# A three-part transformer layer on eight cores: another order of VectorE, ScalarE and GpSimd around feed-forward 1, and of P1 in the output projection

## The reference

```python
# feed-forward (1 and 3)
x_prev = concatenate([zeros, x[:, :-1]], axis=1)
xr = mu_r * x + (1.0 - mu_r) * x_prev
xk = mu_k * x + (1.0 - mu_k) * x_prev
r = sigmoid(xr @ W_r.T)
k_act = square(relu(xk @ W_k.T))
out = r * (k_act @ W_v.T)
# attention block: layer norm, low-rank Q, K, V, causal softmax, then
h = hidden_states + ctx @ out_U @ out_V + out_b
x2 = layernorm(h, ln2_g, ln2_b)
out = h + gelu(x2 @ fc1_U @ fc1_V + fc1_b) @ fc2_U @ fc2_V + fc2_b
```

## Time and profile before

| | |
|---|---|
| median of three runs | 1157.29 us (1156.97 to 1312.77) |
| the profiled execution | 1159.1 us, span of its slowest core (2) 1157.5 us |
| spans of the cores 0 to 7 | 1153.5, 1150.0, 1157.5, 1153.0, 1152.4, 1152.4, 1154.3, 1148.9 us |
| mean granted TensorE clock, core 2 | 0.979 |
| busy on core 2 | TensorE 1051.0 us, VectorE 531.0, ScalarE 534.1, GpSimd 190.6 |
| chain that ended last | TensorE 78%, VectorE 8%, ScalarE 6%, issue 3%, DMA 2% |
| feed-forward 1, first K matmul to last V matmul | 27.88 to 215.2 us |
| projection, OP0 to the last F | 625.4 to 721.1 us |

### The profile page before, as it was taken

One profiled execution on the slowest core, in us unless ns is written; L12 is line 12 of the kernel. 1 busy time (PEld: TensorE's weight loads), 2 busy tenths in 40 slices (PEclk: granted clock), 3 DMA queues, 4 the chain that ended last, 5 costly groups with the idle time before them and its releaser, 6 DMA issues.

```text
span 1157.5 us, 15164 instructions; the slowest of 8 cores (1148.9 to 1157.5 us)
## 1 busy us (share of the span) xinstructions
PE 1051.0 (91%) x5500; PEld 445.6 (38%) x5500; DVE 531.0 (46%) x1011; ACT 534.1 (46%) x646; POOL 190.6 (16%) x189
## 2 busy tenths in 40 slices
PE   1997799999899898888998988999999999999995
PEld 1443344433333333333433433444444444444442
DVE  6466685554544435455467944003021125744511
ACT  2425434356667677777655324333333354241320
POOL 2030321300000002110012213691000000033113
PEclk9999899999999999999998988999999999999998
DMA  8964247712110107540058845973030014131211
GB/s 165 206 179 124 47 120 155 160 24 55 19 19 1 19 1 109 84 64 1 1 165 200 113 68 83 205 150 73 1 73 1 1 37 77 34 109 73 55 55 72
DMA packets 89733, 92.60 MB, mean 80 GB/s; under 512 B 66112, under 2 KB 70336, under 8 KB 88384
## 3 DMA queue, kind: packets, MB, share of 16 engines
q0 software_dynamic: 20112, 52.74, 24.7%
q1 hardware_dynamic: 69552, 38.92, 13.7%
HBM read 91.94 MB, written 16.78 MB: 94 GB/s over the span
## 4 chain that ended last, share of the span: by engine, by line
PE 78%; DVE 8%; ACT 6%; issue 3%; DMA 2%; SPq 1%; POOL 1%; POOLq 0%; ACTq 0%; DVEq 0%
PE ub L865 10%; PE db L1335 9%; PE db L1301 9%; PE db L352 9%; PE db L366 8%; PE db L378 8%; PE ct L1029 5%; PE sd L994 5%; ACT AT L1004 4%; PE db L1273 4%; PE ub L873 3%; PE db L1314 2%; PE db L1288 2%; PE ub L913 2%; DVE st L417 2%
## 5 line engine op out<-in xcount | busy, mean ns | idle before, releaser
L1004 ACT ACTIVATE AT<-sd 128x1024 bf16<-128x1024 f32 (+1 forms) x320 | 265.0, 900 | 126.6 <-PE sd L994 126.5
L1384 ACT ACTIVATE HM<-db,csts 128x512 bf16<-128x512 f32 x128 | 80.7, 684 | 138.9 <-PE db L1301 138.9
L994 PE MATMUL sd<-Qr,Kr 64*128 64x512 bf16 (+3 forms) x640 | 95.3, 349 | 33.8 <-ACT AT L1004 33.2
L1335 PE MATMUL db<-HM,f2U 128*128 128x512 bf16 x512 | 120.3, 379 | 1.6 <-ACT HM L1384 1.6
L1301 PE MATMUL db<-P,f1V 128*128 128x512 bf16 x512 | 120.3, 379 | 0.1
L1029 PE MATMUL ct<-AT,VA 128*64 128x512 bf16 (+3 forms) x640 | 90.1, 359 | 6.1 <-DVE AT L1011 5.9
L1335 PEld LDWEIGHTS db<-HM,f2U 128*128 128x128 bf16 x512 | 49.8, 98 | 62.6 <-issue 3.3
L1301 PEld LDWEIGHTS db<-P,f1V 128*128 128x128 bf16 x512 | 49.9, 98 | 60.9 <-issue 0.8
L1273 PE MATMUL db<-Wo,CN 128*128 128x512 bf16 x256 | 64.1, 417 | 9.8 <-ACT P L1372 9.7
L378 PE MATMUL db<-wv,KAa 128*128 128x512 bf16 x256 | 57.5, 386 | 15.3 <-DVE tta L406 15.3
L1472 DVE CAST P<-db 128x1024 bf16<-128x1024 f32 x4 | 4.9, 1225 | 138.4 <-PE db L1335 138.4
(11 more groups left out here) (153 smaller groups left out, 1306.5 us busy)
## 6 DMA issues: line engine op xcount, KB each, us to landing
S<-xs POOLq DMA_DIRECT2D x32, 512.0 KB, 11.1
xs<-X SPq DMA_DIRECT2D x4, 2048.0 KB, 9.5
x_out<-S SPq DMA_DIRECT2D x16, 512.0 KB, 2.6
wr<-wrT POOLq DMA_DIRECT2D x4, 1024.0 KB, 18.0
X<-x_in SPq DMA_DIRECT2D x2, 2048.0 KB, 14.0
f1V<-fc1V POOLq DMA_DIRECT2D x16, 256.0 KB, 4.0
f2U<-fc2U POOLq DMA_DIRECT2D x32, 128.0 KB, 6.8
X<-x_in SPq DMA_DIRECT2D x4, 512.0 KB, 7.8
```

The source lines that it names most:

```text
L994: m = pe.matmul(SD[q % 2][:, TB * s + off:TB * (s + 1)], Kr[p % 2][64 * s:64 * s + 64, 128 * i:128 * (i + 1)], Qr[p % 2][64 * s:64 * s + 6 ...
L1004: act.activation(c3(AT[q % 4])[:, :, off:TB], c3(SD[q % 2])[:, :, off:TB], AF.Exp, scale=0.125)._wait_ge(a_qk, q + 1).then_inc(a_exp, 1)
L1335: m = pe.matmul(DB[2 + p2 // 2][:, TB * (p2 % 2):TB * (p2 % 2 + 1)], f2U[ic // 8][:, 512 * (ic % 8) + 128 * p2:512 * (ic % 8) + 128 * (p2 ...
L1384: m = act.activation(HM[i % 4][:, TB * e:TB * (e + 1)], DB[job_db[("H", b, i)]][:, TB * e:TB * (e + 1)], AF.Gelu_apprx_tanh, bias=scol("fc ...
```

## The change

- Feed-forward 1: `tt` gets a third buffer, and `dve_kv` waits for the add three tiles back rather than two. kv(b,0) goes ahead of the mixing of the next block, kv(b,1) into `dve_mix_k`, kv(b,2) between the mixings, kv(b,3) into `dve_mix_r`, in all of blocks 0 to 2. Statistics A of block b+1 go between the squares of block b, statistics B of block b-1 behind them, for b = 1 and 2.
- ScalarE: the A rows of block 3 move from among the relus of block 2 to behind its second sigmoid; the B rows of block 1 with them.
- GpSimd: the adds of blocks 1 and 2 wait for XK of the next block, as those of block 0 already did. The loads of the merges move from block 3 to block 2 (when R(2) is done), without the wait for XR(3).
- TensorE: 14 matmuls of the identity with the first columns of `wk0`, into DB0, behind the first transposes.
- `dve_aff1(0)` keeps its place behind the mixings of block 3.
- Projection: ScalarE runs `act_p1` directly behind the rows of tile 7, 11 and 15, ahead of the deviation of the next tile; VectorE takes the scale of tile 7 (11, 15) directly behind the tile itself.

```diff
-    f0.tt = [at("tta%d" % i, 1024, F32, 176 + 4 * i) for i in range(2)]
+    f0.tt = [at("tta%d" % i, 1024, F32, (176, 180, 192)[i]) for i in range(3)]
...
-        n = 4 * b + t
-        if n >= 2:
-            dve.wait_ge(F.add, n - 1)
+        n, k = 4 * b + t, len(f.tt)
+        if n >= k:
+            dve.wait_ge(F.add, n - k + 1)
...
-    def dve_mix_r(dve, F, f, b):
+    def dve_mix_r(dve, F, f, b, kv=None):
...
+        if kv:
+            dve_kv(dve, F, f, b - 1, kv)
         dve.tensor_tensor(XR[:, :, 1:TB], XR[:, :, 1:TB], Z[:, :, 0:TB - 1],
...
+        pe.wait_ge(t_ev, 1)
+        pe.wait_ge(d_wk[0], 16)
+        for i in range(14):
+            pe.matmul(DB[0][:, 0:TB], ident[:, :], wk0[:, 0:TB], start=True, stop=True)
...
+            for p in range(4):
+                act_relu(act, F0, f0, b, p)
+            if b < NB - 1:
+                act_sig(act, F0, f0, b, 0)
+                act_sig(act, F0, f0, b, 1)
                 act_sd_a(act, b + 1)
                 act_z(act, "A", b + 1, range(4))
+                if b:
+                    act_sd_b(act, b - 1)
+                    act_z(act, "B", b - 1, range(4))
+                act_sig(act, F0, f0, b, 2)
+                act_sig(act, F0, f0, b, 3)
...
+        for b in range(1, NB - 1):
             for p in range(4):
                 dve_sq(dve, F0, f0, b, p)
+                dve_stats_a(dve, b + 1, p)
+            for k in range(4):
+                if k == 2:
+                    dve_rs_a(dve, b + 1)
+                dve_stats_b(dve, b - 1, k)
+            dve_rs_b(dve, b - 1)
+            dve_kv(dve, F0, f0, b, 0)
+            for k in range(4):
+                dve.wait_ge(d_tr[k], 16 * (group("A", b + 1) + 1))
+            dve_mix_k(dve, F0, f0, b + 1, kv=1)
+            dve_kv(dve, F0, f0, b, 2)
+            dve_mix_r(dve, F0, f0, b + 1, kv=3)
+            if b == 2:
+                dve_aff1(dve, 0)
...
-                if b == 3 and t == 0:
+                if b == 2 and t == 0:
                     pool.wait_ge(F0.r, 12)
                     pool.dma_start(qVT[:, :], dram["qVT"]).then_inc(d_qV, 16)
                     pool.dma_start(kVTb[:, :], dram["kVTb"]).then_inc(d_kV, 16)
                     pool.dma_start(vVT[:, :], dram["vVT"]).then_inc(d_vV, 16)
-                    pool.wait_ge(F0.xr, 4)
                     pool_pair_weights(pool, 0)
+                if b == 3 and t == 0:
                     pool.wait_ge(F0.k, 16)
...
-                if b == 0 and t == 0:
-                    pool.wait_ge(F0.xk, 2)
+                if b < NB - 1 and t == 0:
+                    pool.wait_ge(F0.xk, b + 2)
...
-            if t + 1 < NT:
+            border = t in (7, 11, 15)
+            if not border:
                 act_op_sd(act, t + 1)
-            if t in (8, 12):
-                act_p1(act, t // 4 - 2)
             act_zu(act, t, (o_nm, t + 1), t, rsC, nmC)
-        act_p1(act, 2)
+            if border:
+                act_p1(act, t // 4 - 1)
+                if t + 1 < NT:
+                    act_op_sd(act, t + 1)
...
-            if t:
+            if t and t not in (8, 12):
                 dve_op_rs(dve, t - 1)
             if t >= 2 and t + 6 < NT:
                 dve_hs(dve, t + 6)
-        dve_op_rs(dve, NT - 1)
+            if t in (7, 11, 15):
+                dve_op_rs(dve, t)
```

More of the change, by code:

```diff
@@ L401, in dve_kv @@
     def dve_kv(dve, F, f, b, t):
-        n = 4 * b + t
-        if n >= 2:
-            dve.wait_ge(F.add, n - 1)
+        n, k = 4 * b + t, len(f.tt)
+        if n >= k:
+            dve.wait_ge(F.add, n - k + 1)
         dve.wait_ge(F.sig, n + 1)
-        dve.scalar_tensor_tensor(f.tt[t % 2][:, :], DB[2 * t % 4 + 1][:, :], 0.5, f.rt[t % 2][:, :],
+        dve.scalar_tensor_tensor(f.tt[n % k][:, :], DB[2 * t % 4 + 1][:, :], 0.5, f.rt[t % 2][:, :],
                                  ALU.mult, ALU.mult)._wait_ge(F.v, n + 1).then_inc(F.kv, 1)
@@ L410, in pool_add @@
         xt = f.x(4 * b + t)
-        pool.tensor_tensor(xt, xt, f.tt[t % 2][:, :],
+        pool.tensor_tensor(xt, xt, f.tt[(4 * b + t) % len(f.tt)][:, :],
                            ALU.add)._wait_ge(F.kv, 4 * b + t + 1).then_inc(F.add, 1)
@@ L650, in act_phase0 @@
         for b in range(NB):
[L651 to L668, removed]
+            for p in range(4):
[3 more added lines that the diff above has]
+                act_sig(act, F0, f0, b, 1)
                 act_sd_a(act, b + 1)
                 act_z(act, "A", b + 1, range(4))
[L671 to L674, removed]
+                if b:
[3 more added lines that the diff above has]
+                act_sig(act, F0, f0, b, 3)
+            else:
+                act_sd_b(act, b - 1)
+                act_sig(act, F0, f0, b, 0)
+                act_z(act, "B", b - 1, [0, 1])
+                act_sig(act, F0, f0, b, 1)
+                act_z(act, "B", b - 1, [2, 3])
                 act_va(act, 0)
-            act_sig(act, F0, f0, b, 2)
-            act_sig(act, F0, f0, b, 3)
+                act_sig(act, F0, f0, b, 2)
+                act_sig(act, F0, f0, b, 3)
         act_sd_b(act, NB - 1)
@@ L701, in dve_phase0 @@
         dve_mix_r(dve, F0, f0, 0)
-        for b in range(NB):
+        for p in range(4):
+            dve_sq(dve, F0, f0, 0, p)
+        for k in range(4):
+            dve_stats_a(dve, 1, k)
+        dve_rs_a(dve, 1)
+        dve_kv(dve, F0, f0, 0, 0)
+        for k in range(4):
+            dve.wait_ge(d_tr[k], 16 * (group("A", 1) + 1))
+        dve_mix_k(dve, F0, f0, 1, kv=1)
+        dve_kv(dve, F0, f0, 0, 2)
+        dve_mix_r(dve, F0, f0, 1, kv=3)
+        for b in range(1, NB - 1):
             for p in range(4):
@@ L706, in dve_phase0 @@
                 dve_sq(dve, F0, f0, b, p)
[L707 to L748, removed]
@@ L749, in dve_phase0 @@
-            if b == 0:
-                dve_mix(dve, 1, dve_mix_r)
+                dve_stats_a(dve, b + 1, p)
+            for k in range(4):
+                if k == 2:
[3 more added lines that the diff above has]
+            dve_kv(dve, F0, f0, b, 0)
+            for k in range(4):
+                dve.wait_ge(d_tr[k], 16 * (group("A", b + 1) + 1))
+            dve_mix_k(dve, F0, f0, b + 1, kv=1)
+            dve_kv(dve, F0, f0, b, 2)
@@ new lines, in dve_phase0 @@
+            dve_mix_r(dve, F0, f0, b + 1, kv=3)
+            if b == 2:
+                dve_aff1(dve, 0)
+        b = NB - 1
+        for p in range(4):
+            dve_sq(dve, F0, f0, b, p)
+            if p < 3:
+                dve_stats_b(dve, b - 1, p)
+            if p == 2:
+                dve_stats_b(dve, b - 1, 3)
+        dve_rs_b(dve, b - 1)
+        dve_aff1(dve, b - 2)
+        for u in early:
+            dve_unit(dve, u)
+        dve_aff1(dve, b - 1)
+        for t in range(4):
+            dve_kv(dve, F0, f0, b, t)
+            if t:
+                dve_stats_b(dve, b, t - 1)
@@ L758, in dve_phase0 @@
             dve_unit(dve, u)
[L760 to L763, removed]
     F0.hz = sem("f0_hz")
```

## The result

The changed kernel takes 1146.56 us (median of the runs; before 1157.29), a ratio of 0.9909 with an interval of 0.989 to 0.9929: 10.7 us faster, where 18.2 were forecast, and just outside the range. The medians are over all executions; the ratios leave out those in which the cores of one die ran slower at a lower granted clock. The profiled execution took 1146.03 us; its slowest core is core 4, span 1144.5 (spans of the eight: 1134.2 to 1144.5).

A forecast was written before the change was run, and what follows sets the result against it. TensorE is busy 1051.0 of 1157.5 us, so only its stands and half-clock time can be won. Feed-forward 1's 3.4 plus the projection's 14.8 take 18.2 off 1157.3: forecast 1139 us, bounds 1127 to 1146.

The forecast's parts named there:

- what comes in its place: Feed-forward 1: new per-block chain and block 3's wait leave a gain of 3.4 us, not 17.6; merge loads cost 0.3.
- Rival (c): Clock falls 2.8 us before V0 (2.9) and block 3's transposes land 2.4 later beside loads: 1144 us, chance 0.11.
- the exclusion: Feed-forward 1: two-input bf16 VectorE sum and GpSimd add exclude each other; XR ready T+14.7 (T: XK ready), otherwise T+12.3.
- the period: Feed-forward 1: each block's chain, from XK ready to the next, takes 43.0 us (41.4 without the exclusion), TensorE's 41.44.
- the wait for G's eviction: Block 3: merges wait for VectorE's evictions of G, R(3,2) at 188.5; stand of about 9 us, slow clock taken 2.3.
- the projection: Projection: P1 is out before OP10 and OP14 need it, so two stands and slow matmuls go: 15.0 us, taken as 14.8.
- the old kv wait: Feed-forward 1: V(1,2) finds kv(1,0) done, so its 15.3 us stand and 1.5 us of slow matmuls go.
- the warm-up: Before K0: fourteen matmuls make K0 and R0 end 2.9 us earlier, but V0 waits for wv, so gain 0.2.
- (a): Feed-forward 1: two-input sums and GpSimd don't exclude one another; period 41.4, gain 9.1 + 14.8: 1133.4 us, chance 0.24.
- (b): Feed-forward 1: GpSimd's adds cost VectorE next to nothing; R(3,2) waits 1.5, gain 16.1 + 14.8: 1126 us, chance 0.09.
- (e): Projection: P1 still waits at the borders, held by something other than its place; 3.4 gained alone: 1154 us, chance 0.03.
- (d): Everywhere: a denser TensorE stream is granted a lower clock; 1.7% pays back the 18.2, 3% gives 1170 us, chance 0.03.

The follow-up runs named there:

- e3: Changed kernel with GpSimd held until block 3's four A transposes have landed before it issues the five merge loads: 1134.83 us, ratio 0.9812.
- the halves: Projection edits alone on the kernel before: 1140.91 us, ratio 0.9865; changed kernel with the projection's old order: 1160.2 us, ratio 1.0025.
- e7: e3 with VectorE's evictions of G, qb and Wq ahead of the affines of blocks 0 and 1: 1129.56 us, ratio 0.9773.
- e1: Kernel before with only the projection edits (borders in ScalarE's and VectorE's order): 1140.91 us, ratio 0.9865.
- e9: e7 with three of a block's four GpSimd adds waiting for XR, and without the fourteen warm-up matmuls: 1124.03 us, ratio 0.9721.
- e6: Changed kernel with one merge load (qVT) beside block 3's A transposes and four held behind them: 1137.7 us, one execution.
- e5: Changed kernel with three merge loads beside block 3's A transposes and two held behind them: 1143.11 us, one execution.
- e10: e7 with three of a block's four GpSimd adds waiting for XR, and 28 warm-up matmuls for 14: 1124.71 us, ratio 0.9726.

## Why the prediction was wrong, and where it was right

**The step that failed** is in the paragraph on what comes in its place: "plus 0.3 for the loads of the merges, five issues that POOL now makes at the end of R2 beside the last transposes". The place and the collision were seen; the size was wrong. It measured 11.2 us at the end (e3). On core 4, 10.5 of them stand in the rows: 8.9 us of later transposes and mixing and 2.8 us of slow matmuls in V(2,3), less the 1.16 that K3 waited in e3. V3 starts 10.0 later there, 10.5 in the mean of the cores (204.9 against 194.4). Rival (c) had the same collision at 2.4 us, and its other half (V0) at 2.9; its 1144 is the nearest to the result, and its two sizes were off as well: the transposes' 2.4 was 6.0 to issue (12.44 against 6.46) and 8.9 to the start of the mixing. The step priced the loads as issues on GpSimd's queue (2.8 us for five), not as traffic beside a latency-bound chain. It also followed the delay to XK(3) alone. The delay reached TensorE before that, at V(2,3), through kv(2,1), which the change itself had put inside that mixing: on core 4 V(2,3) starts at 162.64, and K3, behind it at 168.92, finds XK(3) ready since 167.16. The trace shows this path; no run took kv(2,1) out of the mixing, so how much of the 11.2 it adds over a late XK(3) alone is not measured.

**The sum** from forecast to result: 18.2; projection 0.6 more than its 14.8; the loads 11.2 less; and 3.1 more, which is what remains, to 10.7. It is good to some 2 us, the difference left open between the halves. The remainder is in block 3, where V3 starts 3.3 us ahead of the forecast once the loads are gone. e3 is the prediction's own case without the loads, and on core 2, for which it was worked out, step by step, it reads:

| step of the prediction | forecast | core 2 of e3 |
|---|---|---|
| XK(3) ready, T3 | 157.4 | 157.44 |
| XR ready (exclusion, T+14.7) | 172.1 | 171.70 |
| G out (T+30.5) | 187.9 | 186.86 |
| R(3,2) | 188.5 | 187.50 |
| V3 starts | 197.9 | 194.62 |

**Confirmed**: the exclusion, and by it the period; the wait for G's eviction. **Mis-sized**: the 2.3 us of slow clock behind G. The timeline of TensorE there:

```profile
171.95 3.61 PE L366 MATMUL db<-wr,XRa 128*128 128x512 bf16 x16 [0.29 <-DVE XRa L481]
178.33 0.61 PE L829 MATMUL ub<-kVTb,qVT 128*128 128x128 bf16 x8 [2.76 <-ACT krla L387]
178.77 5.30 PE L366 MATMUL db<-wr,XRa 128*128 128x512 bf16 x16
186.52 0.34 PE L834 MATMUL ub<-bcst,kVTb 128*128 128x1 bf16 x8 [2.44 <-DVE Gs L915]
187.22 0.38 PE L844 MATMUL ub<-Gs,qUT 128*128 128x128 bf16 x4 [0.36 <-DVE qbias L917]
187.50 3.61 PE L366 MATMUL db<-wr,XRa 128*128 128x512 bf16 x16
```

The stop is in two parts, 2.76 before G and 2.44 before qb. The clock fell in the first, the slow 16 matmuls (5.30 for 3.61) ran inside the time in which TensorE would have waited for G anyway, and R(3,2) was at full pace. Lateness of R(3,2) against an undisturbed K3 is 8.2 us, forecast 9; the clock cost nothing on this core, nor on cores 3 and 6. On the other five cores of e3, the two slowest among them, R(3,2) itself was slow, at 4.7 to 5.3 for 3.61: 1.1 to 1.7 us, still under the 2.3. The changed kernel is like those five on seven cores: on core 4 the second stop is 4.13, and R(3,2) behind it was slow.

**Right**: the projection (15.4 measured alone, 15.0 worked out, 14.8 taken); the old kv wait gone; the warm-up worth 0.2 at most, with wv as the bound on the six cores where V0 waits for it. Only the reason was too kind: K0, forecast 2.9 shorter, stays slow on six cores, two of which never wait for wv, since the fall comes back in the stand behind the matmuls; so that the term came out is in part luck. And V0's own slow matmuls, taken as none, came on two cores. "The shortest stand after which the clock fell was 2.7" misreads its trace: 2.7 us is how long TensorE had stood when the clock fell, in a stand of 4.51. Nor is it a bound: on core 2 of the changed kernel V0 takes 15.65 behind a stand of 2.19, and in e7 matmuls are slow behind 1.33. **Rivals**: (a) falls with the halo sum's 2.22 us beside an add, (b) with the scalings, 7.22 beside three adds and 3.00 beside one; (e) falls with e1; (d) has nothing for it, the full stages are at 13.98. e9, without the waits of blocks 2 and 3, comes near (b)'s 1126 by another way.

**Best version**: e9 (the projection's new order; the loads behind the transposes; the merges' evictions first; one add beside the scalings; no warm-up) at 1124.03, by the ratios 32 us under the kernel before and 22 under the change; without the edit of e9 it is the same within the intervals.

What stays open: why a load of 256 KB costs the transposes 0.9 to 1.2 us. On core 4 of the changed kernel the DMA share is 1.03 to 1.28 in each microsecond from 149 to 154; but in e3 it is 1.04 and 1.01 from 146 to 148 too, with the transposes alone in flight, so it is full either way. The five loads write 1.3 MB, and at the 120 to 198 GB/s moved from 149 to 154 that is 7 to 11 us, an estimate from these rows; the mixing was 8.9 late. Shared engines would fit, but that is argued: no run changed the size of a load or its source with the number held, so engines, memory, GpSimd's issuing and the order of descriptors are not told apart. Adds wholly behind XR were not tried either.

## What to carry to other kernels

Price a moved load by what it runs beside, not by its issue: if a transfer that a serial chain waits for is in flight at that time, carry the time that the loads take to land as the bound (here 6.5 to 11.2 us from issue, of which the chain lost 8.9), and hold the load until the chain's transfer has landed if its own reader has slack. An edit that puts an eviction inside a chain of work hands every delay of that chain to the reader of the eviction: after such a move, ask of each wait in the chain what it would do to TensorE's banks. And a slow clock behind a stop costs only what isn't waited for right afterwards.

## What the runs showed of the hardware

- Four DMA transposes leave SyncE's queue within 6.3 us by themselves (e3), and within 7.2, 9.3 and 11.7 us beside one, three and five loads of 256 KB from GpSimd's queue (e6, e5, the changed kernel).
- An 8-column bf16 sum of VectorE takes 0.2 us alone and 2.22 behind a GpSimd add that reads SBUF; a square with two inputs 0.64 to 0.68 alone and 1.05 to 1.41 beside such adds.
- The granted clock's half level (0.50 of full, 1.2 GHz) came after stands of quite different length: after 2.19 us on core 2 of the changed kernel, after 1.33 and 0.36 us on four cores of e7 and not on the other four, and not after 3.15 (e10) or, in front of K0, 3.88 us (changed kernel). The length of one stand alone doesn't say whether the clock falls.
- The warm-up matmuls don't all run at half clock: 14 took 4.1 to 5.2 us in the changed kernel, not the forecast's 6, and 28 took 6.7 to 8.3. The granted clock reads 1.00 all through them, as it does through the slow K0 of the kernel before (16.84 us), so that early in an execution the slow level shows in the matmuls' durations and not in that column.
